# Delta rule kernel: lower and upper blocks sent separate ways, and each head's first two projections placed in the turn

## What is computed

```python
q = l2norm(short_conv(h @ Wq, conv_wq)); k = l2norm(short_conv(h @ Wk, conv_wk)); v = short_conv(h @ Wv, conv_wv)
def step(S, inp):
    qt, kt, vt, gt, bt = inp
    S = S * jnp.exp(gt)
    delta = (vt - kt @ S) * bt
    S = S + kt[:, None] * delta[None, :]
    return (S, qt @ S)
```

## Time and profile before

| what | value |
|---|---|
| median of 3 runs | 1906.04 us (1903.03 to 1913.22) |
| the profiled execution | 1909.25 us, its span 1907.3 us |
| busy in the span: PE, DVE, ACT, POOL | 79%, 56%, 35%, 34% |
| granted clock of PE, mean | 0.909 |

### The profile page before, as it was taken

One profiled execution on the slowest core, in us unless ns is written; L12 is line 12 of the kernel. 1 busy time (PEld: TensorE's weight loads), 2 busy tenths in 40 slices (PEclk: granted clock), 3 DMA queues, 4 the chain that ended last, 5 costly groups with the idle time before them and its releaser, 6 DMA issues. The chain is left out here.

```text
span 1907.3 us, 27547 instructions
## 1 busy us (share of the span) xinstructions
PE 1498.7 (79%) x10473; PEld 1019.4 (53%) x10524; DVE 1060.4 (56%) x2369; ACT 661.8 (35%) x1308; POOL 652.3 (34%) x1049
## 2 busy tenths in 40 slices
PE   4787787777959996857589988899889987488782
PEld 3354544444536664423456766566665676365572
DVE  3856556455223453758367766776777642145652
ACT  3062251431513222544145444453445432022112
POOL 3020110300000000015568666776668672111343
PEclk8999899898969997979799999999999986598996
DMA  1000000000030003231222333214321221421355
GB/s 54 1 1 1 23 2 1 23 1 1 13 90 12 23 11 109 95 85 39 62 52 40 66 78 79 44 36 78 78 64 33 55 45 28 126 87 64 80 120 136
DMA packets 223876, 97.08 MB, mean 51 GB/s; under 512 B 166905, under 2 KB 212386, under 8 KB 223746
## 3 DMA queue, kind: packets, MB, share of 16 engines
q1 hardware_dynamic: 212306, 80.88, 17.6%
q0 software_dynamic: 5376, 12.59, 2.6%
q10 hardware_dynamic: 6064, 1.86, 0.4%
HBM read 63.48 MB, written 31.82 MB: 50 GB/s over the span
## 5 line engine op out<-in xcount | busy, mean ns | idle before, releaser
L1773 POOL TENSOR_TENSOR d_prod<-d_blk 64x30 f32<-64x30 f32 (+4 forms) x360 | 191.5, 532 | 188.3 <-DMA d_blk<-mid_a_blk 161.0
L1805 DVE SCALAR_TENSOR_TENSOR d_conv<-d_prep,k_cw,d_conv 128x511 f32<-128x511 f32 (+2 forms) x288 | 214.5, 746 | 32.5 <-ACT d_conv L1657 25.6
L1777 POOL TENSOR_TENSOR d_blk<-d_blk,d_prod 64x30 f32<-64x30 f32 (+4 forms) x360 | 204.9, 569 | 28.2
L1463 PE MATMUL d_prep<-k_hT,k_w 128*128 128x512 f32 x384 | 189.0, 616 | 24.2 <-POOL d_power L1755 12.9
L424 ACT ACTIVATE a_probs<-a_acc 128x896 f32<-128x896 f32 x128 | 117.1, 918 | 172.6 <-PE a_acc L248 109.7
L523 DVE TENSOR_REDUCE a_top<-a_turn 128x4 f32<-128x512 f32 (+3 forms) x240 | 147.8, 652 | 49.9 <-PE a_turn L210 40.5
L1492 PE MATMUL d_prep<-d_kq 128*128 128x256 f32 x384 | 101.1, 403 | 47.5 <-DVE d_AT L1848 24.8
L471 POOL TENSOR_TENSOR a_rstd<-a_rstd,a_mhalf 128x4 f32<-128x4 f32 x4 | 4.1, 1028 | 372.5 <-DVE a_rstd L575 372.5
L1463 PEld LDWEIGHTS d_prep<-k_hT,k_w 128*128 128x128 f32 x384 | 68.3, 197 | 85.5 <-issue 48.5
L1657 ACT ACTIVATE d_conv<-d_prep,k_cw 128x512 f32<-128x512 f32 x96 | 66.0, 687 | 135.1 <-PE d_prep L1463 134.5
L1492 PEld LDWEIGHTS d_prep<-d_kq 128*128 128x128 f32 x384 | 67.8, 193 | 82.4 <-DVE d_AT L1848 37.5
(11 more groups left out here) (353 smaller groups left out, 3346.6 us busy)
## 6 DMA issues: line engine op xcount, KB each, us to landing
d_alpha<-mid_alpha SPq DMA_DIRECT2D x48, 256.0 KB, 3.9
mid_gate<-p_gate SPq DMA_DIRECT2D x4, 768.0 KB, 3.4
mid_v<-p_v_tok SPq DMA_DIRECT2D x4, 768.0 KB, 3.7
d_v_h<-mid_v SPq DMA_DIRECT2D x12, 256.0 KB, 5.3
d_gate_h<-mid_gate SPq DMA_DIRECT2D x12, 256.0 KB, 4.7
mid_a_blk<-d_AT SPq DMA_DIRECT2D x48, 64.0 KB, 3.4
d_blk<-mid_a_blk SPq DMA_DIRECT2D x12, 256.0 KB, 3.5
mid_u_blk<-d_blk SPq DMA_DIRECT2D x12, 256.0 KB, 2.9
```

The lines of the kernel that those rows point to most:

```text
L1463: last = nc.tensor.matmul(PB[f % 2][:], w[:, n % 2, i, k, :], hT[:, k, b * T:(b + 1) * T], start=k == 0, stop=k == CK - 1)
L1773: nc.gpsimd.tensor_tensor(pr, blk[:, 0:t, t:t + 1].broadcast_to([lanes, t, m]), blk[:, t:t + 1, t + 1:BLK].broadcast_to([lanes, t, m]), AL ...
L1777: nc.gpsimd.tensor_tensor(blk[:, 0:t, t + 1:BLK], blk[:, 0:t, t + 1:BLK], pr, ALU.subtract).then_inc(subst, 1)
L1805: ins = nc.vector.scalar_tensor_tensor(dst, PB[f % 2][:, 0:T - j], cw[:, n % 2, f % 2, TAPS - 1 - j:TAPS - j], dst, ALU.mult, ALU.add)
```

## The change

The inverse: POOL writes -1 on the diagonal of the blocks before the substitution, so that the two negating passes give ones there, and the two fills and the wait at the end go. `inverted` is split: `turned_l` after the transposed pass, `inverted` after the in-place pass. SP stores the lower blocks as soon as they are written, then the upper ones, waits for the lower alone, reads back the four L32 diagonals, and only then the four U32 diagonals; `level2_x` waits for the lower, `level2_l` for the upper ones. Two instead of three decay loads stand before `spread_blocks`.

The order: `project(q + 1, 0)` and `project(q + 1, 1)`, with ACT's and DVE's `convolve` of both, stand in the turn: on PE before `level2_x`, on ACT before `keep_x2`, on DVE before `keep_l`. In `recur` the projections move up by two, so the fourth step has none: there PE has `turn_sums(n + 2, 0)` and `correlate(n + 2, 0)`, which was in the turn.

```diff
             def gather_blocks(n):
+                sp.wait_ge(turned_l, n + 1)
+                sp.dma_start(l_blk.rearrange("j c s t -> (j c) (s t)"), blkT[:].rearrange("p s t -> p (s t)")).then_inc(l_out, 16)
                 sp.wait_ge(inverted, n + 1)
-                sp.dma_start(u_blk.rearrange("j c s t -> (j c) (s t)"), blk[:].rearrange("p s t -> p (s t)")).then_inc(inv_out, 16)
-                sp.dma_start(l_blk.rearrange("j c s t -> (j c) (s t)"), blkT[:].rearrange("p s t -> p (s t)")).then_inc(inv_out, 16)
-                sp.wait_ge(inv_out, 32 * n + 32)
+                sp.dma_start(u_blk.rearrange("j c s t -> (j c) (s t)"), blk[:].rearrange("p s t -> p (s t)")).then_inc(u_out, 16)
+                sp.wait_ge(l_out, 16 * n + 16)
                 if n:
                     sp.wait_ge(l2_e, BATCH * n)
...
-                    sp.dma_start(U32[r, :, r], u_blk[j, :, :, :].rearrange("c s t -> s c t")).then_inc(inv_back, 16)
-                    sp.dma_start(L32[r, :, r], l_blk[j, :, :, :].rearrange("c s t -> s c t")).then_inc(inv_back, 16)
+                    sp.dma_start(L32[r, :, r], l_blk[j, :, :, :].rearrange("c s t -> s c t")).then_inc(l_back, 16)
+                sp.wait_ge(u_out, 16 * n + 16)
+                for j in range(NB):
+                    r = slice(BLK * j, BLK * (j + 1))
+                    sp.dma_start(U32[r, :, r], u_blk[j, :, :, :].rearrange("c s t -> s c t")).then_inc(u_back, 16)
...
-                    load_decays(n + 3, range(BATCH - 1))
+                    load_decays(n + 3, range(2))
                 if n + 2 < D_H:
                     spread_blocks(n + 2)
                 if n + 3 < D_H:
-                    load_decays(n + 3, range(BATCH - 1, BATCH))
+                    load_decays(n + 3, range(2, BATCH))
...
@@ PE: project, correlate, level2, turn, recur
                 elif n:
-                    pe.wait_ge(attn, 8 * n)
+                    pe.wait_ge(attn, 8 * n - 1 + f)
...
+                pe.wait_ge(silued, 8 * n + 2 * b + 2)
                 if f < 2:
-                    pe.wait_ge(conved, 8 * n + 8)
-                    pe.wait_ge(silued, 8 * n + 8)
+                    pe.wait_ge(conved, 8 * n + 7 + f)
...
                 if i == 0:
-                    pe.wait_ge(inv_back, 16 * 2 * NB * (n + 1))
+                    pe.wait_ge(l_back, 16 * NB * (n + 1))
...
             def level2_l(n, i):
+                if i == 0:
+                    pe.wait_ge(u_back, 16 * NB * (n + 1))
...
-                    correlate(q, 0)
+                    if q < 2:
+                        correlate(q, 0)
...
+                if q + 1 < D_H:
+                    project(q + 1, 0)
+                    project(q + 1, 1)
                 if 0 <= m < D_H:
                     for i in range(BATCH):
                         level2_x(m, i)
...
-                        project(n + 2, 2 * c)
+                        if c < 3:
+                            project(n + 2, 2 * c + 2)
+                        else:
+                            turn_sums(n + 2, 0)
...
-                        project(n + 2, 2 * c + 1)
+                        if c < 3:
+                            project(n + 2, 2 * c + 3)
+                        else:
+                            correlate(n + 2, 0)
                         if c == 2:
                             sum_squares(n + 2, 0)
-                        if c == 3:
-                            turn_sums(n + 2, 0)
...
@@ ACT: recur, turn
-                    if ahead:
-                        convolve(n + 2, 2 * c)
-                        convolve(n + 2, 2 * c + 1)
-                if not ahead:
-                    keep_out(n, CH - 1)
+                    if ahead and c < 3:
+                        convolve(n + 2, 2 * c + 2)
+                        convolve(n + 2, 2 * c + 3)
+                if ahead:
+                    keep_sums(n + 2, 0)
+                    silu(n + 2, 7)
+                    square(n + 2, 3)
+                keep_out(n, CH - 1)
...
+                if q + 1 < D_H:
+                    begin(q + 1)
+                    convolve(q + 1, 0)
+                    convolve(q + 1, 1)
+                if 0 <= m < D_H:
                     for i in range(BATCH):
                         keep_x2(m, i)
...
@@ POOL: substitute
-                done = steps * n
+                done = steps * n + 1
+                nc.gpsimd.memset(blk[:].rearrange("p s t -> p (s t)")[:, 0:BLK * BLK:BLK + 1], -1.0).then_inc(subst, 1)
...
-                nc.gpsimd.tensor_scalar(blkT[:].rearrange("p t s -> p s t"), blk[:], -1.0, 0.0, ALU.mult, ALU.add)
-                nc.gpsimd.tensor_scalar(blk[:], blk[:], -1.0, 0.0, ALU.mult, ALU.add).then_inc(subst, 1)
-                pool.wait_ge(subst, done + 1)
-                nc.gpsimd.memset(blk[:].rearrange("p s t -> p (s t)")[:, 0:BLK * BLK:BLK + 1], 1.0)
-                nc.gpsimd.memset(blkT[:].rearrange("p s t -> p (s t)")[:, 0:BLK * BLK:BLK + 1], 1.0).then_inc(inverted, 1)
+                nc.gpsimd.tensor_scalar(blkT[:].rearrange("p t s -> p s t"), blk[:], -1.0, 0.0, ALU.mult, ALU.add).then_inc(turned_l, 1)
+                nc.gpsimd.tensor_scalar(blk[:], blk[:], -1.0, 0.0, ALU.mult, ALU.add).then_inc(inverted, 1)
...
@@ DVE: recur, turn
-                            convolve(n + 2, 2 * c - 1)
+                            convolve(n + 2, 2 * c + 1)
...
-                    if ahead:
-                        convolve(n + 2, 2 * c)
+                    if ahead and c < CH - 1:
+                        convolve(n + 2, 2 * c + 2)
...
                     take_sums(n + 2, 0)
-                    convolve(n + 2, 7)
                 take_out(n, CH - 1)
...
                     finish(n)
+                if q + 1 < D_H:
+                    convolve(q + 1, 0)
+                    convolve(q + 1, 1)
                 if invert:
                     for i in range(BATCH):
                         keep_l(m, i)
```

More of the change, by code:

```diff
@@ L1341, in layer1_delta_rule @@
         (consts, proj, scaled, conved, silued, squared, summed, nsum_ready, n_turned, n_half, n_ready, pow_ready,
-         decayed, kk, attn, blk_out, blk_in, subst, inverted, inv_out, inv_back, k_turned, k_ready, x2, x2_e,
+         decayed, kk, attn, blk_out, blk_in, subst, turned_l, inverted, l_out, u_out, l_back, u_back, k_turned, k_ready, x2, x2_e,
          l2, l2_e, u2, u2_e, x3, x3_e, u3, u3_e, from_k, from_q, r_ready, fs_ready, solved, eps_ready, added, s_ready, s_dec,
@@ L1345, in layer1_delta_rule @@
             "consts", "proj", "scaled", "conved", "silued", "squared", "summed", "nsum_ready", "n_turned", "n_half",
-            "n_ready", "pow_ready", "decayed", "kk", "attn", "blk_out", "blk_in", "subst", "inverted",
-            "inv_out", "inv_back", "k_turned", "k_ready", "x2", "x2_e", "l2", "l2_e", "u2", "u2_e", "x3", "x3_e", "u3", "u3_e",
+            "n_ready", "pow_ready", "decayed", "kk", "attn", "blk_out", "blk_in", "subst", "turned_l", "inverted",
+            "l_out", "u_out", "l_back", "u_back", "k_turned", "k_ready", "x2", "x2_e", "l2", "l2_e", "u2", "u2_e", "x3", "x3_e", "u3", "u3_e",
             "from_k", "from_q", "r_ready", "fs_ready", "solved", "eps_ready", "added", "s_ready", "s_dec", "o_ready",
@@ L1402, in gather_blocks @@
             def gather_blocks(n):
+                sp.wait_ge(turned_l, n + 1)
+                sp.dma_start(l_blk.rearrange("j c s t -> (j c) (s t)"), blkT[:].rearrange("p s t -> p (s t)")).then_inc(l_out, 16)
                 sp.wait_ge(inverted, n + 1)
-                sp.dma_start(u_blk.rearrange("j c s t -> (j c) (s t)"), blk[:].rearrange("p s t -> p (s t)")).then_inc(inv_out, 16)
-                sp.dma_start(l_blk.rearrange("j c s t -> (j c) (s t)"), blkT[:].rearrange("p s t -> p (s t)")).then_inc(inv_out, 16)
-                sp.wait_ge(inv_out, 32 * n + 32)
+                sp.dma_start(u_blk.rearrange("j c s t -> (j c) (s t)"), blk[:].rearrange("p s t -> p (s t)")).then_inc(u_out, 16)
+                sp.wait_ge(l_out, 16 * n + 16)
                 if n:
                     sp.wait_ge(l2_e, BATCH * n)
+                sp.sem_inc(sp_carrier)
                 for j in range(NB):
                     r = slice(BLK * j, BLK * (j + 1))
-                    sp.dma_start(U32[r, :, r], u_blk[j, :, :, :].rearrange("c s t -> s c t")).then_inc(inv_back, 16)
-                    sp.dma_start(L32[r, :, r], l_blk[j, :, :, :].rearrange("c s t -> s c t")).then_inc(inv_back, 16)
+                    sp.dma_start(L32[r, :, r], l_blk[j, :, :, :].rearrange("c s t -> s c t")).then_inc(l_back, 16)
[3 more added lines that the diff above has]
+                    sp.dma_start(U32[r, :, r], u_blk[j, :, :, :].rearrange("c s t -> s c t")).then_inc(u_back, 16)
             def store(n):
@@ L1423, in _ @@
                 load_gate(n)
-            load_decays(1, range(BATCH - 1))
+            load_decays(1, range(2))
             spread_blocks(0)
-            load_decays(1, range(BATCH - 1, BATCH))
+            load_decays(1, range(2, BATCH))
```

(28 more changed lines are left out.)

## The result

The changed kernel took 1884.95 us (median of four, 1879.0 to 1888.92); the kernel before, run beside it, 1904.53. The ratio is 0.9886, 95% interval 0.9844 to 0.9929: 20 to 22 us faster where 31 had been forecast. The profiled execution took 1887.04 us with a span of 1885.3, 22.0 less than the span of before.

A forecast was written before the change was run, and what follows sets the result against it. SP's loop through POOL's inverse was taken to bound the old kernel; PE's would bound the new at 58.8 us. Ten periods save 21.8, two ends 4.4 each: 1906.0 - 30.6 gives 1875 us, range 1860 to 1893.

The forecast's parts named there:

- The ends: First and last inversions, which wait for POOL alone: each gains 4.4 us from the earlier lower blocks.
- SP's loop: Loop from POOL's substitution through SP's stores, gathers and loads to the next block: 57.5 us per head, formerly 60.98.
- PE's loop: PE's work and waits per head: 57.2 us, or 58.8 with collision and clock, so PE sets the period.
- 3.8 gained, 3.9 paid back: On PE, the third correlation comes 3.8 us earlier; two projections ahead of the inverse cost 3.9.
- the half collision: DVE's earlier gate meeting POOL's passes: 0.7 us per head, with ends 0 and 1.4.
- the clock's term: PE's clock drop from idle ahead of the third correlation: half a drop, 0.9 us per head, ends 0 and 1.8.
- fits into the wait: PE's fourth-step work without projections, under 3 us, fits into its wait for DVE's eps; the step gains 1.6 us.
- fifth case: Slower: PE's thin work in fourth step and turn brings four clock drops a head, period 64.4, 1931 us; chance 0.05.
- the prediction's signs of being wrong: Included PE waiting inside the inverse, L1918 over 2 us, several low-clock stretches per head, read-back still ending PE's wait.
- second case: Every head has both the gate's collision and the clock drop: period 60.4, 1891 us; chance 0.20.
- the move buys work inside the transfer's wait: Two projections ahead of PE's inverse, 3.9 us, give PE work while it waits for the transfer.

The follow-up runs named there:

- filled_both: The changed kernel plus products nobody reads, one in the fourth step and two ahead of the third correlation; 1864.12 us, ratio 0.978 to the kernel before.
- the repeat: The changed kernel run again without any edit, in another batch; 1891.26 us, ratio 0.9912 to the kernel before.
- split_only: The kernel before plus only the inverse's edits (separate block stores and read-backs, two decay loads first), projections unmoved; 1872.14 us, ratio 0.9829.
- split_again: The same kernel as split_only, run once more in another batch; 1867.97 us, ratio 0.9814 to the kernel before.
- move_only: The kernel before plus only the two projections moved into the turn and first correlation into the fourth step; 1910.73 us, ratio 1.0023.
- filled_step4: The changed kernel plus two products nobody reads in the fourth step, ahead of turning the norms; 1894.1 us, ratio 0.9932 to the kernel before.
- gate_late: The changed kernel with DVE's gate behind the weighing, value scaling and last product behind the inverse's copies; 1883.69 us, ratio 0.9879 to the kernel before.

## Why the prediction was right, and where not

**The ends.** Forecast 4.4 each. The first inverse gained 5.2, but 0.9 of it is POOL's start (880.1 instead of 881.0); from there to the first product it gained 4.3. The last interval gained only 1.1: head 10's inverse already starts at 1521.73, 1.2 us ahead of the end of the weighing that releases head 11 (1522.9), as no projections stand in that turn, where before the read-back held it to 1.2 us behind (1541.49 against 1540.3). Counted from the end of the weighing, the first product of head 11 comes after 51.3 us instead of 54.8.

**SP's loop.** Forecast 57.5. In the changed kernel it is hidden. In filled_both, where SP never waits for the weighing, POOL's first operations go from 880.1 to 1452.5 in ten heads: 57.2. By terms there: issue to first gather 2.96 (3.4 taken), the gathers 4.26 (4.11), the decay loads 1.76 (1.07), spread to block load 4.49 (4.4). Changed kernel, SP's issues and POOL's passes in a clean head:

```profile
1328.83 0.46 SPq L1404 DMA_DIRECT2D mid_l_blk<-d_blkT  x1
...
1338.96 1.95 SPq L1397 DMA_DIRECT2D mid_a_blk<-d_AT  x4
```

```profile
1326.45 2.35 POOL L1800 TENSOR_SCALAR d_blkT<-d_blk 64x1024 f32<-64x1024 f32 x1
1328.68 1.48 POOL L1801 TENSOR_SCALAR d_blk<-d_blk 64x1024 f32<-64x1024 f32 x1
```

The lower blocks' issue stands 0.03 us behind the end of the transposed pass (0.1 taken). The spread is issued as soon as the weighing has ended (1338.9), in all ten heads, so PE sets the period, as forecast.

**PE's loop.** "3.8 gained, 3.9 paid back" nearly held: from the end of eps to the third correlation it is 7.8 us (1323.78 to 1331.53) instead of 10.9, so 3.1 gained with a collision of 0.8 in it, and 3.7 paid back. The last product of the step starts right behind eps (1323.87 after DVE's 1323.50 and 0.28), the SiLU's wait is gone, the two projections stand ahead of the inverse at 3.67 us, and ACT's and DVE's convolutions hid in their cover. The collision came on the small operation beside L1918's counterpart, not on that one:

```profile
1326.23 0.69 DVE L1934 TENSOR_TENSOR d_o_out<-d_o 128x512 f32<-128x512 f32 x1
...
1327.67 0.98 DVE L1938 SCALAR_TENSOR_TENSOR d_mean<-d_mean,d_eps_q 128x16 f32<-128x16 f32 x1
```

0.98 us where filled_both has 0.17: 0.8 lost in each of the four clean heads, against the half collision of 0.7. It ended at 1328.65, POOL's transposed pass at 1328.80. By the rule of the Trainium skill (SBUF — State Buffer, "Who interferes with whom") this operation, with two inputs in SBUF, would have been blocked until the pass was done and have taken some 1.3 us; the trace has less, as it had for L1918. The collision isn't new: in the kernel before, the same small operation took 0.97 to 1.57 us in four of the ten heads. Loop and collision were forecast at 57.9; clean heads measured 57.6 to 58.0.

**The failed step: the clock's term.** "Half a drop, 0.9" stood between two ends for one place, the idle ahead of the third correlation. Measured, the mean period lies 59.5 - 57.8 = 1.7 above the clean one, 0.6 of it from the first head's 64.2; in the repeat, (1534.0 - 927.2) / 10 = 60.7, it lies 2.9 above. A head with falls in both places costs some 3.4. Half of the falls lie where the prediction saw no price: it wrote that what PE has in the fourth step "fits into the wait", and booked the loss of the projections there as a gain of 1.6 us alone. Its fifth case named this mechanism, but with four falls a head, and at 0.05; the chip showed none to two. Several low stretches in a head were among the prediction's signs of being wrong, and four of the ten heads had two. Of the 9.7 us between the forecast's sum of 30.6 and the 20.9 in the profile, 7.2 are ten periods of 59.53 instead of 58.8; the last interval lacks 3.3, and the first inverse gives 0.8 back. The median of 1885 lies 10 us above the forecast and 6 below the second case (1891), and the repeat at 1891.26 on that case; neither describes the heads, which differ among themselves. That the range held both runs is owed in part to its width.

**Which part gains.** The prediction held that the move buys work inside the transfer's wait. It priced the move with the old wait in place; after the split there is no such wait, for split_only has none in the ten heads. The split alone gains all that the change gains and, by the medians of two runs of each, more (split_only, split_again; one pair of the intervals overlaps), the move alone nothing (move_only). By the ratios, from other batches, the changed kernel and its repeat lie 0.0057 to 0.0098 above the two runs of the split, 11 to 19 us: so much the move takes back. The profiles divide it: ten periods take 595.2 us in the changed kernel and 575.5 in split_only. The clean heads differ by 0.6 each (57.8 against 57.2), so some 6 of the 19.7 us are the collision and the wait for the weighing, and the rest lies in the heads with a low clock. filled_both, which keeps the move, adds only unread work and returns it all, agrees with that, but can't separate the two: its fill also shifts the gate and the norms out of POOL's passes. What picks the heads in which the clock falls stays open: with the same instructions the two profiles had four clean heads and one.

filled_both and split_again beat both kernels; between the two (0.978 and 0.9814, overlapping intervals) nothing is decided, and split_again is the simpler kernel.

## What to carry to other kernels

When two edits aim at the same wait, price each with the other already in: the split had removed the wait that the move was to fill. Taking projections out of a stretch of narrow, dependent products had a price of its own here, though nothing in that stretch waited longer: look at the granted clock of such a stretch by heads, not at the idle time alone. Unread products are a quick test of it. One place filled alone (filled_step4) gained nothing, as the falls came at the other; both filled gained 20 us and more.

## What the runs showed of the hardware that was not expected

The clock fell to 1.2 GHz in the fourth step without any idle of over 0.63 us just ahead of it, while PE ran 32-column products and transposes back to back (eight products 1.76 us instead of 0.98). Adding 2.9 us of products per head took 21 to 27 us off the kernel (1864.12 against 1884.95 and 1891.26, in other batches). And VectorE operations on 128x16, 0.17 us by themselves, took 0.66 to 0.98 in the lines shown beside GpSimd's 64x1024 passes, as much as a 128x512 operation costs alone (0.69), and up to 1.75 in other heads of gate_late.
